# Attention and mixture-of-experts block on one core: the router's weights of pairs 4 to 16 are spread by transfers and multiplied on GpSimd

## The reference, cut to what matters

```python
logits = x @ Wr + br                              # 1024 tokens, 32 experts
aff = sigmoid(logits)
top_v, top_i = top_k(aff, 8)
w_full[t, top_i] = top_v / (sum(top_v) + 1e-9)    # zero for the others
shared = (silu(x @ Wg_s + bg_s) * (x @ Wu_s + bu_s)) @ Wd_s + bd_s
gate = silu(x @ Wg[e] + bg[e]);  up = x @ Wu[e] + bu[e]     # 64 wide, each e
down = (gate * up) @ Wd[e] + bd[e]
out = x + shared + sum_e w_full[:, e] * down[e]
```

## Time and profile before

| | us |
|---|---|
| median of 3 runs | 268.4 |
| the profiled execution's own time | 269.61 |
| its span (first to last instruction) | 267.8 |
| TensorE matmuls busy | 236.1 (88%) |
| VectorE busy | 184.5 (69%) |
| ScalarE busy | 134.3 (50%) |
| GpSimd busy | 65.4 (24%) |

### The profile page before, as it was taken

One profiled execution on the slowest core, in us unless ns is written; L12 is line 12 of the kernel. 1 busy time (PEld: TensorE's weight loads), 2 busy tenths in 40 slices (PEclk: granted clock), 3 DMA queues, 4 the chain that ended last, 5 costly groups with the idle time before them and its releaser, 6 DMA issues.

```text
span 267.8 us, 3680 instructions
## 1 busy us (share of the span) xinstructions
PE 236.1 (88%) x1216; PEld 163.5 (61%) x1225; DVE 184.5 (69%) x450; ACT 134.3 (50%) x272; POOL 65.4 (24%) x104
## 2 busy tenths in 40 slices
PE   8989999999785659899997778887799999999993
PEld 2547454644552126686886456664578888888871
DVE  2698976924548867772442646877978888888883
ACT  2358487785229501523432357647555555555551
POOL 6235700203052100000840210300035353534100
PEclk9999999999589988999999999979999999999998
DMA  7990000000000000000240000000011212110002
GB/s 240 427 382 26 0 0 1 2 0 2 0 0 0 0 4 0 0 0 2 80 119 2 0 0 2 1 0 0 0 42 39 79 42 71 50 39 0 2 0 78
DMA packets 5140, 11.61 MB, mean 43 GB/s; under 512 B 801, under 2 KB 1921, under 8 KB 4866
## 3 DMA queue, kind: packets, MB, share of 16 engines
q1 hardware_dynamic: 4290, 10.61, 11.6%
q10 hardware_dynamic: 832, 0.78, 1.0%
HBM read 10.86 MB, written 0.52 MB: 43 GB/s over the span
## 4 chain that ended last, share of the span: by engine, by line
PE 72%; DVE 17%; ACT 6%; issue 3%; POOL 1%; DVEq 0%; ACTq 0%; POOLq 0%
PE bank L1742 5%; PE bank L1739 5%; PE bank L1738 5%; PE bank L1167 5%; PE bank L1300 4%; PE bank L1286 4%; DVE att L645 4%; PE bank L1241 4%; PE bank L1771 3%; PE bank L1624 3%; PE bank L1768 3%; PE bank L1193 3%; PE bank L1614 3%; PE bank L1751 3%; PE bank L1769 3%
## 5 line engine op out<-in xcount | busy, mean ns | idle before, releaser
L1132 ACT ACTIVATE arena_d<-bank,bias 128x512 f32<-128x512 f32 x34 | 23.4, 688 | 33.3 <-PE bank L1742 33.2
L810 DVE SCALAR_TENSOR_TENSOR arena_d<-bank,bias,arena_d 128x512 f32<-128x512 f32 x34 | 25.5, 751 | 10.5 <-ACT arena_d L1132 10.3
L501 DVE TENSOR_REDUCE smax<-bank 128x3 f32<-128x462 f32 (+2 forms) x44 | 25.4, 619 | 5.9 <-PE bank L1241 5.6
L1738 PE MATMUL bank<-arena_b 128*128 128x512 f32 x68 | 27.2, 400 | 0.3 <-DVE arena_d L819 0.3
L1742 PE MATMUL bank<-arena_b 128*128 128x512 f32 x68 | 27.0, 397 | 0.0
L1739 PE MATMUL bank<-arena_b 128*128 128x512 f32 x68 | 26.9, 396 | 0.0
L936 ACT ACTIVATE arena_c<-bank 128x512 f32<-128x512 f32 x40 | 22.6, 597 | 7.1 <-PE bank L1286 3.3
L407 POOL CAST arena_b<-rec 128x512 fp32r<-128x512 f32 x17 | 13.5, 794 | 50.3 <-PE bank L1771 50.2
L824 DVE TENSOR_TENSOR arena_a<-arena_d,arena_a 128x512 fp32r<-128x512 f32 x34 | 23.2, 682 | 0.7 <-ACT arena_a L1139 0.7
L707 DVE TENSOR_SCALAR arena_a<-bank,pack 128x512 fp32r<-128x512 f32 x16 | 12.0, 751 | 16.0 <-PE bank L1606 13.3
L1139 ACT CAST arena_a<-arena_d 128x512 fp32r<-128x512 f32 x34 | 20.8, 612 | 3.6 <-DVE arena_d L819 2.3
(11 more groups left out here) (244 smaller groups left out, 497.0 us busy)
## 6 DMA issues: line engine op xcount, KB each, us to landing
rec<-in_rec SPq DMA_DIRECT2D x17, 257.0 KB, 2.6
arena_d<-in_fc SPq DMA_DIRECT2D x1, 2048.0 KB, 10.2
fc<-in_fc SPq DMA_DIRECT2D x1, 2048.0 KB, 14.4
x<-in_x SPq DMA_DIRECT2D x2, 256.0 KB, 4.3
out<-x SPq DMA_DIRECT2D x2, 256.0 KB, 2.0
watt<-in_watt SPq DMA_DIRECT2D x1, 384.0 KB, 4.4
pack<-in_pack ACTq DMA_DIRECT2D x1, 382.0 KB, 5.7
ctx<-in_ctx ACTq DMA_DIRECT2D x2, 154.0 KB, 7.0
```

The lines of the kernel that those rows point to most:

```text
L501: dve.tensor_reduce(dst, src, AX.X, ALU.max).then_inc(Z["max_done"], 1)
L810: dve.scalar_tensor_tensor(to[:, k % 2, :], bank[:, 2 + k % 2, :], bias[:, u % SPLITS, 1:2], sil[:, k % 2, :], ALU.add, ALU.mult).then_inc ...
L1132: act.activation(sil[:, k % 2, :], bank[:, k % 2, :], f, bias=bias[:, STEPS[k][0] % SPLITS, 0:1])\
L1738: pe.matmul(d, whi[:, r, w], y3hi[:, cs], start=True, stop=False)
```

## The change

- For steps whose pair is above PICKED = 3 (26 of the 34: k = 6, 8, and 10 to 33) the matmul `router_weights` and the product `weighted` go. In their place SyncE spreads two rows of the turned router weights, kept in full float32 in `wfull` (32 partitions, one expert each), over 64 partitions each, into a ring `wexp` of WSLOTS = 4. GpSimd multiplies `sil` with it (`scale`) to `gu`, and VectorE's one product (up + bias) x gu gives `hh`.
- `wfull` is a new copy by ScalarE for each half (`full_weights`), after high_hidden(0) and after k = 5.
- The low part of the records from n = 6 on is made by VectorE (`low_record`), no longer by GpSimd. The ring of split records grows to 6.
- The up part rotates over 4 banks from step TRIPLE = 10 on, `hhi` and `hlo` have 4 slots, and down(k) follows three steps behind its gate_and_up, not two. The turned router weights of half 0 lie in bank 6, and down(0) waits until they are copied.
- Several loads share one semaphore (`fc`, `last`), and their users wait for all of them.

```diff
-SPLITS = 5
+SPLITS = 6
+PICKED = 3
+WSLOTS = 4
+HSLOTS = 4
+SPREAD = [k for k in range(NSTEP) if STEPS[k][0] > PICKED]
+TRIPLE = max(k for k in range(NSTEP) if 0 < STEPS[k][0] <= PICKED) + 1
@@ sync
-            sp.dma_start(mask[:, :, :], mask_d).then_inc(L["mask"], 16)
+            sp.dma_start(mask[:, :, :], mask_d).then_inc(L["last"], 16)
...
+            def spread(m):
+                u, b = STEPS[SPREAD[m]]
+                sp.wait_ge(Z["wfull_ready"], b + 1)
+                if m >= WSLOTS:
+                    sp.wait_ge(Z["scaled"], m - WSLOTS + 1)
+                for h in range(2):
+                    ex = 2 * (u - 1) + h
+                    sp.dma_start(wexp[h * I1:(h + 1) * I1, m % WSLOTS, :],
+                                 wfull[ex:ex + 1, None, b * S:(b + 1) * S].broadcast_to([1, I1, S]))\
+                        .then_inc(Z["spread%d" % (m % WSLOTS)], 16)
+            for n in range(3, SPLITS + 3):
+                record(n)
+            at = SPLITS + 3
+            for m, k in enumerate(SPREAD):
+                spread(m)
+                if at < PAIRS and k >= 2 * at - 7:
+                    record(at)
+                    at += 1
@@ gpsimd
+            def scale(m):
+                k = SPREAD[m]
+                pool.wait_ge(Z["spread%d" % (m % WSLOTS)], 32 * (m // WSLOTS + 1))
+                pool.wait_ge(Z["sil_ready"], k + 1)
+                pool.wait_ge(Z["hh_ready"], k - 1)
+                pool.tensor_tensor(gu[:, k % 2, :], sil[:, k % 2, :], wexp[:, m % WSLOTS, :], ALU.mult)\
+                    .then_inc(Z["scaled"], 1)
-            for n in range(SPLITS, PAIRS):
-                split(n)
+            for k in range(NSTEP):
+                if k in SPREAD:
+                    scale(SPREAD.index(k))
+                if k % 2 == 0 and SPLITS <= k // 2 + 3 < PAIRS:
+                    split(k // 2 + 3)
@@ vector, gated(k)
+                if k in SPREAD:
+                    dve.wait_ge(Z["scaled"], SPREAD.index(k) + 1)
+                    dve.wait_ge(Z["hlo_ready"], k - 1)
+                    dve.scalar_tensor_tensor(hh[:, k % 2, :], bank[:, up_bank(k), :], bias[:, u % SPLITS, 1:2],
+                                             gu[:, k % 2, :], ALU.add, ALU.mult).then_inc(Z["hh_ready"], 1)
+                    return
+            def low_record(n):
+                r = n % SPLITS
+                dve.wait_ge(Z["bias_ready"], parts_split(n))
+                dve.tensor_tensor(wlo[:, r, :], rec[:, n % 3, 0:3 * P], f32(whi[:, r, :]), ALU.subtract)\
+                    .then_inc(Z["split_ready"], 1)
@@ scalar
+            def full_weights(b):
+                act.wait_ge(Z["w3_ready"], 2 * (b + 1))
+                act.copy(wfull[:, b * S:(b + 1) * S], bank[0:E1, (6, 7)[b], :]).then_inc(Z["wfull_ready"], 1)
@@ tensor
-                if u:
+                if 0 < u <= PICKED:          # router_weights(k)
...
                 pe.wait_ge(Z["w3_ready"], 2 * (b + 1))
+                pe.wait_ge(Z["wfull_ready"], b + 1)   # down_bias(b)
...
-                down(k - 2)
+                if k < TRIPLE:
+                    down(k - 2)
+                elif k > TRIPLE:
+                    down(k - 3)
+            down(NSTEP - 3)
             down(NSTEP - 2)
```

More of the change, by code:

```diff
@@ L166, in build @@
         slotT = slotT.bitcast(BF16)
+        wexp, _, wfull = lay(arena_c, ([P, WSLOTS, 512], [P, 3 * T * E1], [E1, T * P]))
         screp, = lay(arena_c, ([P, T, E0, P // E0],))
@@ L243, in f32 @@
             return ap.bitcast(F32)
-        L = {n: sem("ld_" + n) for n in ("x0", "x1", "ctx2", "watt", "pack", "late", "rows", "gate", "fc1", "fc2", "mask", "wout", "wr", "bd")}
+        L = {n: sem("ld_" + n) for n in ("x0", "x1", "ctx2", "watt", "pack", "late", "rows", "gate", "fc", "last")}
         names = """var_ready rstd_ready consts_ready xn_ready xnT_psum xnT_ready q_psum qhi_ready qlo_ready k_psum
@@ L306, in _, with record @@
                 sp.dma_start(rec[:, n, :], rec_d[n]).then_inc(Z["rec_ready%d" % n], 16)
-            for n in range(3, PAIRS):
+            def record(n):
                 sp.wait_ge(Z["split_ready"], n - 2)
                 sp.dma_start(rec[:, n % 3, :], rec_d[n]).then_inc(Z["rec_ready%d" % (n % 3)], 16)
+            def spread(m):
[16 more added lines that the diff above has]
+                    at += 1
+            assert at == PAIRS
             for b in range(B):
@@ L393, in _ @@
             pool.wait_ge(Z["ylo_ready"], 1)
-            pool.wait_ge(L["bd"], 16)
+            pool.wait_ge(L["last"], 64)
             pool.tensor_copy(bd3[:, :], bd[:, :]).then_inc(Z["bd_ready"], 1)
@@ L615, in _ @@
             maxima(7, 5)
-            dve.wait_ge(L["mask"], 16)
+            dve.wait_ge(L["last"], 64)
             dve.tensor_scalar(keep[:, :, :], mask[:, :, :], 0.0, None, ALU.is_equal).then_inc(Z["keep_ready"], 1)
@@ L808, in gated @@
                 dve.wait_ge(Z["up_psum"], k + 1)
+                if k in SPREAD:
[4 more added lines that the diff above has]
+                    return
                 to = gu if u else hh
-                dve.scalar_tensor_tensor(to[:, k % 2, :], bank[:, 2 + k % 2, :], bias[:, u % SPLITS, 1:2], sil[:, k % 2, :],
+                dve.scalar_tensor_tensor(to[:, k % 2, :], bank[:, up_bank(k), :], bias[:, u % SPLITS, 1:2], sil[:, k % 2, :],
                                          ALU.add, ALU.mult).then_inc(Z["gu_ready" if u else "hh_ready"], 1)
             def weighted(k):
-                if STEPS[k][0]:
-                    n = sum(u > 0 for u, _ in STEPS[:k + 1])
+                if 0 < STEPS[k][0] <= PICKED:
+                    n = sum(0 < u <= PICKED for u, _ in STEPS[:k + 1])
                     dve.wait_ge(Z["upw_psum"], n)
@@ L843, in _ @@
                     low_weights(1)
+                if k % 2 == 0 and SPLITS <= k // 2 + 3 < PAIRS:
+                    low_record(k // 2 + 3)
             low_hidden(NSTEP - 1)
@@ L1136, in high_hidden @@
                 act.wait_ge(Z["hh_ready"], k + 1)
-                if k >= 2:
-                    act.wait_ge(Z["down_done"], k - 1)
-                act.copy(hhi[:, k % 2, :], hh[:, k % 2, :]).then_inc(Z["hhi_ready"], 1)
+                if k >= HSLOTS:
+                    act.wait_ge(Z["down_done"], k - HSLOTS + 1)
+                act.copy(hhi[:, k % HSLOTS, :], hh[:, k % 2, :]).then_inc(Z["hhi_ready"], 1)
             def result(b):
@@ L1513, in _ @@
             score_rows(1)
-            pe.wait_ge(L["wout"], 16)
+            pe.wait_ge(L["last"], 64)
             for b in range(B):
@@ L1661, in _ @@
             idle_work(12, 5)
-            pe.wait_ge(L["wr"], 16)
+            pe.wait_ge(L["last"], 64)
             tile = lambda b, i: slice((b * TB + i) * P, (b * TB + i + 1) * P)
@@ L1736, in gate_and_up @@
                     w = slice(j * P, (j + 1) * P)
[L1737 removed]
+                    d = bank[:, up_bank(k) if j else k % 2, :]
+                    if j and k >= TRIPLE:
+                        pe.wait_ge(Z["hh_ready"], max(TRIPLE, k - 3))
                     pe.matmul(d, whi[:, r, w], y3hi[:, cs], start=True, stop=False)
```

63 lines of the change are left out of this document (39 added, 24 removed).

## The result

The changed kernel takes 403.15 us (median of 4 runs, 401.18 to 403.71) against 268.4 us before: a ratio on record of 1.496, 95% interval 1.489 to 1.503 (the two medians alone give 1.502). The forecast was slower by the transfers, 449 us, with 400 to 465 as that case's own range and 263 to 462 as the whole one. Direction and mechanism held; the size was 46 us too large, which is all but 3 us of what the case's own range allowed, and the whole range was so wide that it held the case of no loss too. Where the 46 us come from is one of the things the experiments show.

The account below looks back on a forecast made before the run. TensorE bound the kernel before; afterwards the transfers would: 26 x 9.75 = 253.5 us from 185.5 to 439.0, product to 440.4, ending to 447.7, clock to 448.7, then + 1.8 - 1.2 = 449 us. Range 263 to 462.

Parts of the forecast that it names:

- slower by the transfers: Spread steps: transfers through a single path bind the kernel, 449 us, own range 400 to 465, chance 0.44.
- The narrow read: Spread transfers: all 16 engines share one path to a router row's partition, 262 KB at 26.9 GB/s, 9.75 us a step.
- The row of a full stretch: Earlier profile, 7 to 14 us: all 16 engines loaded, moving 430 GB/s, 26.9 GB/s each, taken as the single path's rate.
- The step that failed: Spread transfers: assumed no overlap between successive steps' rows, so each step costs the full 9.75 us.
- The share of 1.04: DMA share from 7 to 14 us in the earlier profile, read as packets on an engine hardly overlapping.
- rival B: Spread transfers of neighbouring steps overlap: 4.9 us a step, 323 us; half an overlap 386; chance 0.22.
- the last chain: End of span: 8.5 us from line 810's start, less 1.2 for the other product, plus up to 1.0 for the clock.
- The records: Eight records sharing the transfers' queue: packets of 0.94 us each on other paths, counted at 0, at most 7.5 us.
- The clock: TensorE mostly waiting: if its clock falls to the lower level, the last chain costs up to 1.0 us more.
- Rival A: Spread transfers as cheap as records, TensorE stays the bound at 2.06 us a step: 263.7 us, chance 0.24.
- The terms of TensorE's side: Matmuls taken out: -6.4 us, nine matmuls or 2.06 us a step; down_bias(1) later: +1.5 us.
- Rival C: GpSimd becomes the bound, its products waiting for VectorE's line 824: 2.54 us a step, 275 us; with mixtures, chance 0.06.

Follow-up runs that it names:

- Experiments 1 and 2: Six edits of the changed kernel's spread transfers: HBM row 270.24 us, distinct partitions 270.67, half columns 292.85; same row 403.29, rows 17 apart 322.46, rows 0 to 3 451.95.
- dead product: Changed kernel without transfers, GpSimd's 26 products working on resident y0 with results nobody reads or waits for: 274.19 us, against 263.83 without products.
- experiment 4: Changed kernel with wfull stored to HBM and its rows spread from there: 270.98 us; with the records' low part also back on GpSimd: 276.72 us.

## Why the prediction was right, and where it was off

- *The narrow read.* The prediction assumed that the partition of a router row has one path for all 16 engines and gave it one engine's full rate, 26.9 GB/s or 9.75 us a step. Experiments 1 and 2 show each part: only a row in SBUF is slow, by the byte, and where nothing can overlap the step takes 9.78 us. The row of a full stretch was a good measure for a path that no row showed.
- *The step that failed* is the clause "that in-order packets do not reach past it to the next step's row". The share of 1.04 was read as packets that hardly overlap on an engine. That is so here as well: in the trace's packet records of the changed kernel, from 258 to 384 us, more than 16 packets (one for each engine) are in flight at once in only 0.2% of the time. But it says nothing of 16 engines among each other. In the run on rows 0 to 3 a packet of 2 KB takes 1.09 us in the median and 95% of them over 0.9; in the changed kernel 57% do, and 18% take under 0.15 us. So some engines are already at a row of the next step, which few others read, while the others are still at this one's. (The records don't name the engine of a packet, so this last step is argued.) The changed kernel takes 6.98 us a step without a record and 7.68 in the mean, where 9.75 was forecast: 25 x (9.75 - 7.68) = 52 us too much. Nearly all successive steps read different groups of four rows. The last two don't (rows 28 and 29, then 30 and 31), and together they take 16.0 us, from 374.83 to 390.83, where the two before them take 13.2, from 361.64. The run on rows 0 to 3 alone pays the full price and takes 451.95 us against the 449 forecast. So the truth lay between the forecast case and rival B, which had priced "half an overlap" at 386. That it stayed 3 us inside the case's range was luck: nothing in the forecast bounded the overlap.
- *The rest of the 46 us.* The first product stands at 198.90 us, since it waits for ScalarE's silu, where the forecast had its transfer landed by 195.3. From line 866 at 392.29 us to the end at 401.7 the last chain takes 9.4 us where 8.3 was counted, 1.0 for the clock in it.
- The Trainium skill, "SBUF — State Buffer", section "Door 1: The DMA port swizzle", puts four neighbouring partitions on one port of 27.2 GB/s. The measurements agree, for reading: 26.8 GB/s for partitions 0 to 3, the same time for one row as for two neighbours, and side by side for rows 17 apart.
- *The records* were counted at 0, at most 7.5 us, and this is the second term that was mis-sized. The run on rows 0 to 3 has them at (354.28 - 214.91) / 14 = 9.95 us a step against 9.78, some 2 us in all. In the changed kernel the eight intervals with a record are 9.46 us in the mean and the eight that follow them 6.90: two steps take 16.4 us with a record and 14.0 without, eight times 2.4 or 19 us, which covers the whole difference between 7.68 and 6.98 (25 x 0.70 = 17.5). Their own packets are not slow (0.085 us in the median). The likely cause is that an engine that is ahead spends its lead on the record and not on the next step's row; no run tests it.
- *The clock* fell, as the forecast allowed: the granted clock is 0.60 from 258 to 390 us and 0.50, the lower level, from 380 to 395, with matmuls 0.43 us apart. TensorE waits elsewhere, so this costs only in the last chain.
- *Rival A's sum* was 263.7 us, and the run without transfers and products takes 263.83. The terms of TensorE's side hold: nine matmuls at 2.04 us a step, and down_bias(1) late by 1.4 (195.90 in the changed kernel against 194.45 in the earlier trace rows). The match to 0.1 us is partly luck, since A's last chain has a product of 1.3 us that this run leaves out, and the run's ratio of 0.981 makes it 263.3. And A as a whole was wrong: it took GpSimd's product to fit into 2.06 us without touching VectorE.
- *Rival C* was right in its mechanism and put the loss on one engine. Both lose: in the kernel through HBM GpSimd's product is 1.42 us in the mean and not 1.3, VectorE's subtraction 1.18 and not 0.68. The price of 2.54 us a step was too high for the kernel through HBM (2.24) and too low for the second half of the run without transfers (5.39 us for two steps, 2.70). C had a chance of 0.06 and A 0.24; with cheap transfers the runs fall at 270 to 277 us, so these two should have stood the other way round. The prediction had the evidence in its own rows, 0.61 us for a cast early and 0.89 in the stage, and used it only as the worst case.
- "Who interferes with whom" on the same page of the Trainium skill says that a VectorE instruction with two SBUF inputs and a GpSimd one that reads SBUF block each other. The runs agree: beside a dead product the subtraction takes 1.78 us against 0.68, with no data in common, and beside a copy of one operand either the subtraction (1.05 us) or the copy (1.15 against 0.61) is stretched.

By addition: two steps now read for 2 x 1.29 + 0.50 + 0.19 = 3.27 us on GpSimd (two products, a record's cast and its copy) and 2 x 0.68 + 0.55 = 1.91 on VectorE with two SBUF inputs, 5.18 us against TensorE's 4.12. The measured 4.47 to 5.39 lie around that sum. The 4.47 can lie below it because each instruction in turn gains 0.08 to 0.14 us, as the ends in experiment 4 show. In the kernel before, VectorE's second product took an operand from PSUM, and it wasn't stretched beside GpSimd: of these two

```profile
200.59 0.89 POOL L407 CAST arena_b<-rec 128x512 fp32r<-128x512 f32 x1 [2.71 <-PE bank L1771]
...
200.93 0.68 DVE L819 TENSOR_TENSOR arena_d<-arena_d,bank 128x512 f32<-128x512 f32 x1
```

the second takes the 0.68 us that it takes anywhere. The change put a product with both operands in SBUF, on GpSimd, in its place.

Left open: why the runs without transfers and with dead products go from 4.47 us for two steps to 5.4 at about 225 us and stay there, while the kernel through HBM doesn't; and how far the DMA engines run apart, that is, why a step takes 6.98 us and not less. Neither was tried by itself.

## What to carry to other kernels

A transfer that spreads one SBUF row over many partitions is priced by the row that it reads: bytes written, divided by one engine's rate (26.8 GB/s here), and not by sixteen. That is the price where nothing overlaps; overlap with transfers of other rows took 0.2 to 0.3 of it off. Store the row to HBM once and spread it from there: rows from different groups of four partitions side by side only brought the step from 7.0 to 4.2 us. And before work goes to GpSimd beside a busy VectorE, add up the time of GpSimd's instructions that read SBUF and of VectorE's with two operands in SBUF, as if it were one more engine; if the sum is above the step, the moved work comes back as longer VectorE instructions, where no row of waits shows it.

## What the runs showed of the hardware that was not expected

- Transfers in one queue overlap when their rows lie in different groups of four partitions: 6.98 us a step in the mean of six, where all in one group take 9.78. A record of fast packets between them takes most of that gain away again: 9.46 us for such a step.
- VectorE and GpSimd can bound a step together by reading SBUF in turn: six of their instructions end one behind the other from 225.99 to 229.09 us, and most of it shows as longer instructions.
- SyncE's issue of a transfer, 0.33 us before, takes 3.8 us in the median while the transfers are behind, and holds up what stands behind it: an instruction that only issues also waits.
- A GpSimd copy of 128 x 512 float32 took 0.61 us undisturbed and up to 1.17 beside VectorE's subtraction; a product took 1.26 to 1.30 in the changed kernel, where VectorE mostly waits.
